# VectorE's norm, residual and router steps in smaller parts, and their places in the order of a fused two-layer kernel

## What is computed

```
x = x + tanh(g_xattn[0]) * L0_xattn(layernorm(x), ctx, mask)   # 16 heads, softmax, out projection,
                                                               # scaled, layernorm, gamma and beta
x = x + tanh(g_ffn[0])   * L0_ffn(layernorm(x))                # shared expert + 7 routed, top 3
x = x + tanh(g_xattn[1]) * L1_xattn(layernorm(x), ctx, ctx)    # gated recurrent cell as a masked product
x = x + tanh(g_ffn[1])   * L1_ffn(layernorm(x))                # block-quantised gate, up, down

# L0_xattn, per head:  p = clip(exp(q k / 4)) by key mask; o = (p v) / sum(p)
# L0_ffn:  gate_probas = softmax(x @ gate_w + gate_b)
#          top 3 of gate_probas + biases, weights normalised to sum 1
#          out = expert_shared(x) + sum_e w_e * (silu(x @ W1[e]) * (x @ Wg[e])) @ W2[e]
```

## Time and profile before

| | us |
|---|---|
| median of 3 runs (lowest, highest) | 495.32 (494.81, 496.61) |
| profiled execution, its own time | 496.37 |
| span of that execution | 494.6 |
| TensorE busy (share) | 381.1 (77%) |
| VectorE busy | 349.6 (71%) |
| ScalarE busy | 189.1 (38%) |
| GpSimd busy | 152.8 (31%) |
| chain that ended last: TensorE, VectorE, issue | 49%, 24%, 12% |
| mean granted clock of TensorE | 0.87 |

### The profile page before, as it was taken

One profiled execution on the slowest core, in us unless ns is written; L12 is line 12 of the kernel. 1 busy time (PEld: TensorE's weight loads), 2 busy tenths in 40 slices (PEclk: granted clock), 3 DMA queues, 4 the chain that ended last, 5 costly groups with the idle time before them and its releaser, 6 DMA issues.

```text
span 494.6 us, 6936 instructions
## 1 busy us (share of the span) xinstructions
PE 381.1 (77%) x2330; PEld 258.7 (52%) x2330; DVE 349.6 (71%) x857; ACT 189.1 (38%) x331; POOL 152.8 (31%) x147
## 2 busy tenths in 40 slices
PE   7899787799997697959767887979577478660745
PEld 3566454545556585848545555657353156440323
DVE  4586259257633989887976657577995976789895
ACT  4456424323313122603343545444004577640331
POOL 4029300028425445546325223233212020030240
PEclk9999997579998989979995999999697759966695
DMA  8900000003402203302986930907000670000001
GB/s 280 254 12 0 9 1 1 1 1 107 129 0 65 85 12 122 104 20 88 201 187 89 164 104 0 141 31 107 2 0 0 106 129 1 2 0 1 23 20 45
DMA packets 33714, 32.69 MB, mean 66 GB/s; under 512 B 3876, under 2 KB 32784, under 8 KB 33680
## 3 DMA queue, kind: packets, MB, share of 16 engines
q1 hardware_dynamic: 31088, 28.99, 26.4%
q0 software_dynamic: 992, 1.68, 1.2%
q10 hardware_dynamic: 1600, 1.57, 1.0%
HBM read 28.04 MB, written 4.19 MB: 65 GB/s over the span
## 4 chain that ended last, share of the span: by engine, by line
PE 49%; DVE 24%; issue 12%; ACT 6%; POOL 3%; DMA 3%; SPq 1%; DVEq 0%; ACTq 0%; POOLq 0%
PE bank L869 14%; PE bank L895 6%; PE bank L781 5%; PE bank L797 3%; PE bank L754 3%; PE bank L1005 2%; PE bank L969 2%; DVE mxraw L1610 2%; DVE mam L1452 2%; DVE tok L1262 2%; PE bank L765 1%; PE bank L917 1%; PE bank L954 1%; DVE probs L1537 1%; DMA qrep<-part_dram 1%
## 5 line engine op out<-in xcount | busy, mean ns | idle before, releaser
L895 PE MATMUL bank<-wexp,wT 128*128 128x256 f32 x192 | 53.9, 406 | 7.7 <-DVE x L1444 7.6
L869 PE MATMUL bank<-tok_r,probs_r 128*128 128x512 f32 x104 | 48.0, 462 | 11.6 <-DVE wT L1433 7.0
L1322 DVE TENSOR_SCALAR probs<-probs,hi 128x512 f32<-128x512 f32 x64 | 34.6, 592 | 28.8 <-ACT probs L1077 28.7
L663 POOL TENSOR_TENSOR wexp_r<-wexp,probs_r 128x1024 fp32r<-128x1024 f32 x13 | 31.2, 2403 | 60.3 <-ACT probs_r L1088 60.3
L1127 ACT ACTIVATE silu_sb<-bank 128x512 f32<-128x512 f32 x32 | 19.1, 597 | 77.1 <-PE bank L869 77.1
L1077 ACT ACTIVATE probs<-bank 128x1024 f32<-128x1024 f32 x32 | 32.2, 1025 | 41.1 <-PE bank L781 41.1
L591 POOL TENSOR_TENSOR mx_grid<-parts,bl 128x1024 bf16<-128x1024 fp8e4 x9 | 17.2, 1910 | 96.0 <-DVE parts L1613 96.0
L895 PEld LDWEIGHTS bank<-wexp,wT 128*128 128x128 f32 x192 | 37.1, 203 | 15.3 <-issue 10.5
L1537 DVE SCALAR_TENSOR_TENSOR probs<-bank,dexp 128x384 f32<-128x384 f32 x48 | 26.4, 554 | 24.0 <-PE bank L955 17.7
L869 PE MATMUL bank<-tok_r,wexp_r 128*128 128x512 f32 x104 | 42.7, 411 | 0.0
L781 PE MATMUL bank<-qrep,krep 32*128 32x256 f32 x256 | 35.8, 410 | 1.8 <-issue 1.0
(11 more groups left out here) (261 smaller groups left out, 895.9 us busy)
## 6 DMA issues: line engine op xcount, KB each, us to landing
wexp<-in_L_ffn_W SPq DMA_DIRECT2D x28, 256.0 KB, 4.1
krep<-part_dram SPq DMA_DIRECT2D x32, 128.0 KB, 6.6
qrep<-part_dram SPq DMA_DIRECT2D x32, 128.0 KB, 4.6
wexp<-in_L_ffn_Wg SPq DMA_DIRECT2D x14, 256.0 KB, 4.6
part_dram<-parts POOLq DMA_DIRECT2D x4, 384.0 KB, 3.0
part_dram<-parts SPq DMA_DIRECT2D x4, 384.0 KB, 3.3
x<-in_x ACTq DMA_DIRECT2D x2, 512.0 KB, 7.2
ctx<-in_ctx SPq DMA_DIRECT2D x2, 512.0 KB, 7.0
```

Of the source, the lines that this page charges most:

```text
L663: gp.tensor_tensor(low, raw, w_high[k % 2].bitcast(F32), ALU.subtract).then_inc(s["w_low_ready"], 1)
L869: mm = pe.matmul(bank[:, bk, :], lhs, rhs, start=(kk == 0 and q == 0), stop=(kk == KC - 1 and q == len(terms) - 1))
L895: mm = pe.matmul(bank[:, 2 + pair, D * t:D * t + D], hid[k % 2][m][:, col:col + P], wexp[:, k % WR, 2, m, :], start=(m == 0), stop=(m == 1))
L1322: ins = v.tensor_scalar(w, w, hi[:, 2 * b + kc:2 * b + kc + 1], EM50, ALU.min, ALU.max)
```

## The change

No instruction's work is changed. VectorE's steps are cut up: ln_in keeps the statistics and ln_root gets the inverse root; delta_in gives its root to delta_root; delta_out gives its first pass to delta_mid; route keeps its first three instructions, route_rank has the softmax and the comparisons, route_weigh the rest; VectorE's part of score becomes a step clamp of its own, directly behind score everywhere but in groups 4 and 5. There all eight score steps come ahead of the clamps, with delta_mid, delta_out, ln_in 2, ln_root 2 and ln_out 2 between them; values 4 comes behind gate 0. x_split 0 moves ahead of the experts on ScalarE, and on GpSimd ahead of the copies of the gate weights and of the context. The woven chains have more and smaller side steps, so that delta_in 1, ln_in 3, ln_in 4, cell_in 0, cell_mid 0, cell_out 0 and ln_in 6 come up to one TensorE step earlier, and the roots, route_rank 1 and route_weigh 1 later. cell_in 0 thereby comes ahead of w_split 15, which has parts on ScalarE and GpSimd as well.

```
@@ -123,7 +123,7 @@
     st = lambda name, *ix: [(name, i) for i in (ix or (0,))]
-    plan = st("key_masks") + st("ln_in", 0) + st("turn", 0, 1, 2) + st("bias_turn") + st("project", 0) + st("turn", 3)
+    plan = st("key_masks") + st("ln_in", 0) + st("ln_root", 0) + st("turn", 0, 1, 2) + st("bias_turn") + st("project", 0) + st("turn", 3)
     plan += st("ln_out", 0) + st("project", 2) + st("turn", 4, 5) + st("mask_turn") + st("project", 1)
@@ -137,7 +137,7 @@
         if g - 1 >= first:
             late[1] = late[1] + st("values", g - 1)
             late[2] = st("values_copy", g - 1)
-        return [st("score", 4 * g + j) + late[j] for j in range(4)]
+        return [st("score", 4 * g + j) + st("clamp", 4 * g + j) + late[j] for j in range(4)]
     def attention_end(g):
         w = g // 2
@@ -146,15 +146,15 @@
                 st("turn2", g) + st("turn2_copy", g), st("wo", w)]
     first = attention(0)
-    plan += flat(first[:2]) + st("project", 3) + st("turn", 6, 7) + st("ln_in", 1) + flat(first[2:]) + st("v_project", 0)
+    plan += flat(first[:2]) + st("project", 3) + st("turn", 6, 7) + st("ln_in", 1) + st("ln_root", 1) + flat(first[2:]) + st("v_project", 0)
     plan += st("ln_out", 1) + flat(attention(1)) + st("v_project", 1) + st("tanh")
     plan += weave(attention(2), st("turn", 8, 9)) + weave(attention(3), st("turn", 10, 11))
     end = attention_end(3)
     plan += end[0] + end[1] + st("project", 4) + end[2] + st("project", 5) + end[3] + end[4] + st("project", 6) + end[5]
-    second = [st("project", 7) + st("v_project", 2, 3)] + attention(4, 4) + attention(5, 4) + attention(6, 4)
-    second = [second[q] + second[q + 1] for q in (0, 2, 4, 6)] + second[8:]
-    plan += st("delta_in", 0) + second[0] + st("delta_out", 0) + second[1] + second[2] + st("ln_in", 2) + second[3] + st("ln_out", 2)
-    plan += st("xt", 0) + second[4] + st("route", 0)
+    plan += st("delta_in", 0) + st("delta_root", 0) + st("project", 7) + st("v_project", 2, 3) + st("score", 16, 17)
+    plan += st("delta_mid", 0) + st("delta_out", 0) + st("score", 18, 19) + st("ln_in", 2) + st("score", 20, 21) + st("ln_root", 2)
+    plan += st("ln_out", 2) + st("score", 22, 23) + st("clamp", 16, 17, 18, 19) + st("xt", 0) + st("route", 0) + st("x_split", 0)
+    rest = [st("values", 4) + st("clamp", 20, 21) + st("values_copy", 4) + st("route_rank", 0), st("clamp", 22, 23) + st("route_weigh", 0)]
     def expert(k, mx=None):
@@ -176,11 +176,11 @@
         return now + (st("accumulate", 2 * k - 1) if k else [])
-    plan += weave(flat([expert(k) for k in range(3)]), second[5:] + attention(7, 4) + attention_end(7))
-    plan += st("w_split", 3) + st("x_split", 0)
-    chain = st("delta_in", 1) + st("delta_out", 1) + st("ln_in", 3) + st("ln_out", 3)
+    plan += weave(flat([expert(k) for k in range(3)]), rest + attention(6, 4) + attention(7, 4) + attention_end(7))
+    plan += st("w_split", 3)
+    chain = st("delta_in", 1) + st("delta_root", 1) + st("delta_mid", 1) + st("delta_out", 1) + st("ln_in", 3) + st("ln_root", 3) + st("ln_out", 3)
     plan += weave(expert(3, 0) + expert(4, 1) + expert(5, 2), chain)
-    plan += weave(expert(6, 3), st("xt", 1) + st("route", 1)) + st("x_split", 1) + expert(7, 4)
+    plan += weave(expert(6, 3), st("xt", 1) + st("route", 1)) + st("x_split", 1) + weave(expert(7, 4), st("route_rank", 1) + st("route_weigh", 1))
     def cells(g, first=0):
@@ -205,13 +205,13 @@
         return [st("cell_values", g) + st("cell_values_copy", g), st("turn3", g) + st("cell_normalise", g)]
     def prepare(n):
-        return st("ln_in", 4 + n) + st("ln_out", 4 + n) + st("xt", 2 + n) + st("q_high", 2 * n, 2 * n + 1) \
+        return st("ln_in", 4 + n) + st("ln_root", 4 + n) + st("ln_out", 4 + n) + st("xt", 2 + n) + st("q_high", 2 * n, 2 * n + 1) \
             + st("gate_rows", n) + st("q_split", 2 * n) + st("gate_math", n) + st("q_split", 2 * n + 1)
     def finish(n):
-        return st("cell_in", n) + st("cell_mid", n) + st("cell_out", n) + st("ln_in", 6 + n) + st("ln_out", 6 + n)
-
-    plan += expert(8, 5) + weave(expert(9, 6), prepare(0)[:2] + [[]] + prepare(0)[2:4]) + weave(expert(10, 7)[:6], prepare(0)[4:]) + expert(10, 7)[6:8] + st("turn_gates", 0)
+        return st("cell_in", n) + st("cell_mid", n) + st("cell_out", n) + st("ln_in", 6 + n) + st("ln_root", 6 + n) + st("ln_out", 6 + n)
+
+    plan += expert(8, 5) + weave(expert(9, 6), prepare(0)[:3] + [[]] + prepare(0)[3:5]) + weave(expert(10, 7)[:6], prepare(0)[5:]) + expert(10, 7)[6:8] + st("turn_gates", 0)
     plan += weave(expert(10, 7)[8:] + flat([expert(k, k - 3) for k in range(11, 14)]), flat([cells(g) for g in range(4)]) + cells_end(3))
     plan += weave(expert(14, 11) + expert(15, 12), finish(0))
     plan += st("out", 30, 31) + st("quantise", 0) + st("accumulate", 30, 31)
@@ -234,7 +234,7 @@
         return [now("last", 4, True) + early, part(0), part(1) + late, now("quantise", 0) + now("down", 3, True)]
     ready = prepare(1)
-    plan += st("q_turn", 0) + ready[:2] + flat(stage_d(0)[:3]) + ready[2:] + flat(stage_d(0)[3:]) + st("turn_gates", 1)
+    plan += st("q_turn", 0) + ready[:3] + flat(stage_d(0)[:3]) + ready[3:] + flat(stage_d(0)[3:]) + st("turn_gates", 1)
     plan += flat(stage_d(1) + stage_d(2)[:3])
     plan += weave(flat([cells(g, 4) for g in range(4, 8)]), [[]] + stage_d(2)[3:]) + flat(cells_end(7))
     plan += weave(finish(1), stage_d(3)[:3]) + flat(stage_d(3)[3:])
@@ GpSimd's queue @@
...
                 gp.dma_start(part_dram[1, u].rearrange("a p t -> p a t"), parts[:, u, :, :]).then_inc(s["ck_stored"], 16)
-            gp.wait_ge(s["gate_loaded"], 16 * 14)
...
-            gp.wait_ge(s["pv_done"], 8)
-            for i in range(NT):
-                gp.tensor_scalar(vaug[:, i, 0:H * VS]
...
-            def w_split(k):
...
             def x_split(n):
...
+            x_split(0)
+            gp.wait_ge(s["gate_loaded"], 16 * 14)
...
+            gp.wait_ge(s["pv_done"], 8)
...
+            def w_split(k):
...
@@ -691,7 +692,7 @@
             steps = dict(w_split=w_split, x_split=x_split, mx_quantise=mx_quantise, q_split=q_split, cell_in=cell_in, quantise=quantise)
             for name, i in plan:
-                if name in steps:
+                if name in steps and (name, i) != ("x_split", 0):
                     steps[name](i)
@@ -1250,6 +1251,8 @@
                     m = seq.add(v.bn_aggr(mv[:, i, :], st[:, i, :]))
                 seq.wait(m)
                 seq.add(v.tensor_scalar(ve[:, k, :], mv[:, i0:i0 + TH, 1], LN_EPS, None, ALU.add))
+
+            def ln_root(k):
                 inverse_root(ri[:, k, :], ve[:, k, :], ru[:, 0, :], ru[:, 1, :])
             def ln_out(k):
@@ -1313,7 +1316,7 @@
                 seq.add(v.tensor_tensor(rs2[:, 1:2], rs2[:, 0:1], rs2[:, 0:1], ALU.mult))
                 seq.wait()
-            def score(u):
+            def clamp(u):
                 g, jj = u // 4, u % 4
                 _, _, b, _ = group(g)
                 v.wait_ge(s["exp_done"], u + 1)
@@ -1355,17 +1358,22 @@
                     seq.add(v.bn_aggr(mv[:, i, :], st[:, i, :]))
                 seq.wait()
                 seq.add(v.tensor_scalar(dve_[:, n, :], mv[:, i0:i0 + TH, 1], rs2[:, 1:2], LN_EPS, ALU.mult, ALU.add))
+
+            def delta_root(n):
                 inverse_root(dri[:, n, :], dve_[:, n, :], ru[:, 0, :], ru[:, 1, :])
                 seq.wait()
                 seq.add(v.tensor_scalar(dri[:, n, :], dri[:, n, :], rs2[:, 0:1], None, ALU.mult))
+
+            def delta_mid(n):
+                i0 = TH * n
+                seq.wait()
+                v.wait_ge(s["gscaled"], 2)
+                for i in range(i0, i0 + TH):
+                    seq.add(v.scalar_tensor_tensor(tok[:, i, :], tok[:, i, :], mv[:, i, 0:1], lng[:, :], ALU.subtract, ALU.mult))
             def delta_out(n):
                 i0 = TH * n
-                seq.wait()
-                v.wait_ge(s["gscaled"], 2)
                 v.wait_ge(s["x_beta"], i0 + TH)
-                for i in range(i0, i0 + TH):
-                    seq.add(v.scalar_tensor_tensor(tok[:, i, :], tok[:, i, :], mv[:, i, 0:1], lng[:, :], ALU.subtract, ALU.mult))
                 seq.wait()
                 for i in range(i0, i0 + TH):
                     seq.add(v.scalar_tensor_tensor(x[:, i, :], tok[:, i, :], dri[:, n, i - i0:i - i0 + 1], x[:, i, :], ALU.mult, ALU.add))
@@ -1383,6 +1391,9 @@
                 seq.add(v.tensor_reduce(lgs[:, 0, :], lgt, AX.X, ALU.max))
                 seq.wait()
                 v.tensor_tensor(lg[:, 0, :, :], lgt, bc(lgs[:, 0, :]), ALU.subtract).then_inc(s["rexp_in"], 1)
+
+            def route_rank(n):
+                bc = lambda ap: ap.unsqueeze(2).broadcast_to([P, TH, NE])
                 v.wait_ge(s["rexp_out"], n + 1)
                 seq.add(v.tensor_reduce(lgs[:, 1, :], lg[:, 1, :, :], AX.X, ALU.add))
                 seq.wait()
@@ -1400,6 +1411,9 @@
```

(3 more changed lines are left out.)

61 lines of the change are left out of this document (35 added, 26 removed).

## The result

The changed kernel takes 482.64 us (median of four executions: 479.95, 480.16, 485.13, 485.56) beside 495.4 us before; the ratio is 0.974, with a 95% interval of 0.970 to 0.978. Its profiled execution took 480.16 us (span 478.3), against 496.37 before: 16.2 us less. The forecast was 480.8 for that execution and 479.7 for the median. The total is right; several of the parts are not, as the stretches show.

The account below looks back on a forecast made before the run. No engine bounds everywhere: TensorE from 104.5 to 152 us, VectorE in 159–197.3 and 339.1–365.4 us. Terms 6.4 - 0.5 + 4.0 + 1.5 + 5.4 + 1.4 - 2.6 = 15.6 us saved: 480.8 profiled, 479.7 median, range 471 to 487.

Parts of the forecast that it names:

- A and B: Attention's second end, 73 to 104.5 us: 6.4 us saved (4.4 to 13.5); then to 152 us: 0.5 us lost.
- C: Start of expert 3: x_low ready 2.3 us earlier, clock staying up; 4.0 us saved, 2.3 if the clock falls.
- D1: Experts 3 to 5, 159 to 197.3 us: half of VectorE's idleness goes, 1.5 us saved (4 lost to 5.5 saved).
- D2: Expert 6 and second routing, 197.3 to 216.1 us: TensorE's 5.28 us wait goes, 5.4 us saved (3.3 to 7.2).
- F: At ln_in 4: statistics go ahead of step 18's activation, ln_out 4 ends earlier; 1.4 us saved (0 to 1.7).
- E: cell_in 0 ahead of w_split 15: split queues later and mx_quantise 11 is locked once more; 2.6 us lost (0 to 5).
- The low clock case: Attention's end, main case: TensorE's clock is low, back at 96.0 us, and up ends at 98.1; 6.4 us saved.
- The rival's case: Attention's end: TensorE's clock stays up, 13.5 us saved instead of 6.4, giving 472.6 us; chance 0.18.
- B alone: From 104.5 to 152 us: x_split 0 on GpSimd can hold VectorE's clamps; 0.5 us lost (nothing to 1.2).
- The sign of the last line: Stated sign of being wrong: VectorE still full but its 4-element root operations at 1 to 2 us each, in numbers.
- the lock rival: 159 to 216.1 us: VectorE stands still through GpSimd's operations, 22 us added, 501.7 us at the most; main case keeps 0.51.
- expert gains vanish: VectorE's sum is the bound from 152 to 224 us; D1 and D2 give nothing, E 5: 489.0 us; chance 0.10.

Follow-up runs that it names:

- a_again: The changed kernel run again with nothing altered, for its spread: 486.03 us, ratio 0.982 to the kernel before.
- xsplit_only: The kernel before with x_split 0 alone moved, behind the first routing, on GpSimd ahead of the gate weights: 490.35 us, ratio 0.989.
- attn_only: The changed kernel's attention end and early x_split 0, with the expert chains placed as in the kernel before: 485.69 us, ratio 0.976.
- experts_only: The kernel before with only the changed kernel's new expert chains; old attention end and place of x_split 0: ratio 1.0007.
- combo: Changed kernel with pieces, ranking and weighing moved around GpSimd's runs, ln_in 4, cell_in 0, ln_in 6 in old places, spare TensorE matmuls: 475.28 us, ratio 0.960.
- dodge: The changed kernel with the seven pieces of the chain of experts 3 to 5 moved ahead of mx_grids: 484.82 us, ratio 0.978.
- before_again: The kernel before, unchanged, run once more with its profile: 497.1 us, one execution.
- nolock: The changed kernel without the first two of GpSimd's three operations of mx_quantise 0 to 2, result not right: 477.38 us, one execution.
- combo_nowarm: The same kernel as combo without the spare matmuls: 480.17 us, ratio 0.970.
- warm: The changed kernel with a spare matmul behind each of scores 16 to 23 and four ahead of the router's product: 482.29 us, ratio 0.974.

## Why the prediction was right, and where it was not

| term | forecast | measured, after (a_again) |
|---|---|---|
| A and B | 5.9 saved | 11.3 (6.4) saved |
| C | 4.0 saved | 4.0 (4.0) saved |
| D1 | 1.5 saved | 3.4 (3.4) lost |
| D2 | 5.4 saved | 0.9 (0.9) saved |
| F | 1.4 saved | 0.3 (0.3) lost |
| E | 2.6 lost | 0.6 (0.6) lost |
| in no term | 0 | 4.5 (4.4) saved |
| sum, by the stretches | 15.6 | 16.3 (11.4) saved |

**A and B** were right in mechanism: tok was ready at 81.70 (forecast 81.5), and the transposes waited for the scores alone. The low clock case was right in size: 6.4 in a_again (5.9 forecast). The rival's case was not met in full even by the lucky execution: 11.3 us of the 13.0 (13.5 less 0.5), with the clock still low for 3.4 us. (Halving the stated prices from 79.5 on gives an end at about 90.2, not 91.0, so that case was written 0.8 us too small as well.) What failed is that the clock was taken as one outcome with a chance; it differs from execution to execution. The forecast gave 0.67 to a low clock and 0.18 to a high one; two of ten executions were near 480. The profiled execution that gave 480.16 was of the rarer kind, and 4.5 us came where no term stood; these two together hid the failure of the expert terms. That the total of the profiled execution came out to 0.6 us is luck. The median of 482.64 and a_again's 486.03 are 2.9 and 6.3 us above the forecast. The early VectorE finish did not keep the clock up by itself: the fall at 77.3 us came inside the scores, without TensorE idle for longer than 0.46 us. The prediction tied the fall at 80.1 to TensorE's having stood idle from 79.5; a_again shows a fall without such idleness.

**B alone**: from the exponential of score 24 to step 5 it is 40.45 us against 42.18 before, and gate 1's four products (half of the 3.70 us at 91.32) moved out of it: 0.1 us lost instead of 0.5.

**C** was right to 0.1 us: TensorE's product at 140.59 starts 0.10 us behind the end of w_split 3 (138.14 + 2.35), GpSimd's only operation there. Timeline of TensorE in after:

```profile
140.59 0.47 PE L870 MATMUL bank<-tok_r,probs_r 128*128 128x512 f32 x1 [0.45 <-issue]
```

**D1** failed in one step: "splitting moves such instructions to other places, with the same odds". The idle rest did shrink by half as forecast (3.0 to 1.4 us). But VectorE's busy time grew by 4.9 us, and 4.9 less 1.6 is the 3.3 us lost. The odds were not the same, and could have been worked out from the list: each mx_grids starts GpSimd's run of three operations, and w_split follows it, some 6.2 us (149.78 to 155.91 in after) in which VectorE's operations on SBUF alone were held. The new weave put the root and delta_out behind mx_grids. (With the old order reached as early as in xsplit_only and attn_only, D1 was 39.8 and 40.2 us, so 0.8 to 1.2 us of the loss may belong to the arrival; experts_only has the 3.4 us without it.) The lower bound of the term (4 lost) held. The sign of the last line ("4-element root operations at 1 to 2 us each") is what came.

The Trainium skill, page "SBUF — State Buffer", section "Who interferes with whom", says that whoever comes first gets the shared ports for the whole instruction while the other is blocked entirely, and that the order of issue decides who is blocked, not the shape of the operation. The trace agrees: 128x4 operations took up to 2.24 us, until the GpSimd operation of 2.38 us ended. That rule, which the prediction left to the lock rival (chance 0.05) alone, carried the sign of D1.

**D2** was mis-sized. Timelines of VectorE and TensorE in after, where ranking and weighing went:

```profile
198.10 2.39 DVE L1402 TENSOR_TENSOR lg<-lg,lgs 128x28 f32<-128x28 f32 x1
...
209.46 2.33 DVE L1431 TENSOR_TENSOR cw<-lg,lgs 128x28 f32<-128x28 f32 x1
```
```profile
206.15 0.50 PE L870 MATMUL bank<-tok_r,probs_r 128*128 128x512 f32 x1 [2.50 <-DVE hid_x L1447]
...
213.48 0.50 PE L870 MATMUL bank<-tok_r,probs_r 128*128 128x512 f32 x1 [2.55 <-DVE wT L1447]
```

The wait of 5.28 us became two, of 2.50 and 2.55 us; VectorE's sum is 25.55 us in this stretch, 25.56 before. The estimate of 2 us coming back took the ranking alone and forgot the weighing and its lock. What remains is 0.9 us, with a granted clock of 1.00 instead of 0.89 in the window; the forecast had 2.0 us for the clock. (Its own terms, 7.3 less 2, give 5.3, not 5.4.) The "expert gains vanish" rival, given 0.10, describes the sizes of D1, D2 and F better than the main case did, but not its reason: VectorE's sum did not stay, it grew by the held time. combo put the ranking clear of GpSimd's run (0.19 us for the product of L1402 that took 2.39), and the stretch became no shorter (32.02 us). VectorE in combo:

```profile
180.40 2.31 DVE L1493 TENSOR_SCALAR mx_sc<-mx_top 128x16 f32<-128x16 f32 x1
193.38 2.09 DVE L1482 TENSOR_SCALAR mx_top<-mx_top 128x16 uint32<-128x16 uint32 x1
204.13 2.33 DVE L1436 TENSOR_TENSOR lg<-lg 128x28 f32<-128x28 f32 x1
```

Two operations of mx_quantise and one of the weighing were held instead. Taken together, D1 and D2 are 70.5 us before, 73.0 after, 68.2 in dodge and 67.3 in combo.

**F**: the transposes' wait fell from 1.70 to 0.54 us, as forecast. But the last statistics operation (L1253) was held 2.14 us, and step 18's first product waited:

```profile
220.81 2.14 DVE L1253 TENSOR_SCALAR ve<-mv 128x4 f32<-128x4 f32 x1
```
```profile
223.69 0.47 PE L870 MATMUL bank<-tok_r,probs_r 128*128 128x512 f32 x1 [2.02 <-DVE silu_sb L1441]
...
227.23 1.09 PE L843 MATMUL bank<-identf,tok 128*128 128x128 f32 x8 [0.54 <-DVE tok L1265]
```

**E** went as told: w_split 15 directly behind cell_in's product, and a second lock on mx_quantise 11 beside the one of the earlier trace rows. Timelines of GpSimd and VectorE in after:

```profile
327.68 2.39 POOL L690 TENSOR_TENSOR pvs<-tok,lsc 128x1024 f32<-128x1024 f32 x1 [9.44 <-DVE tok L1583]
330.02 2.35 POOL L673 TENSOR_TENSOR wexp_r<-wexp,probs_r 128x1024 fp32r<-128x1024 f32 x1
```
```profile
328.23 1.87 DVE L1468 TENSOR_SCALAR mx_top<-mx_top 128x16 uint32<-128x16 uint32 x1
330.13 2.27 DVE L1479 TENSOR_SCALAR mx_sc<-mx_top 128x16 f32<-128x16 f32 x1
```

It cost 0.6 us in the stretch, not 2.6. The granted clock was 0.94 there and 0.81 before, so part of the price is hidden under a better clock. The table separates the two: with 3.4 us of low clock in the stretch, the old place took 25.94 to 25.96 us (before_again, xsplit_only, attn_only) and the new one 26.88 to 26.90 (after, a_again, dodge, nolock). The new place thus costs 0.9 us.

**In no term**: from step 21 to 28 after gained 2.3 us with no change of order. The low clock there was 13.7 us long in both executions of before and 6.8 in after. xsplit_only, whose order there is that of before, has 6.8 us too and 72.95 us: so the new order isn't needed for it; that the earlier arrival is what did it was not tested. The other 2.1 us, behind quantise 0, stay open. The first execution of before had 10.2 us of low clock at 397.5 us where after had 3.4; but before_again had 3.4 there as well and still took 126.10 us, so the clock at that place seems to account for some 0.5 us only. Kernels with the new places of cell_in 0 and ln_in 6 take from 124.0 (nolock) to 127.3 us (experts_only) behind quantise 0, those with the old ones 126.1 to 126.8. Why the low stretches fall where they do stays open too.

## What to carry to other kernels

Before VectorE's small SBUF steps are moved, list GpSimd's unbroken runs of operations: of a step inside one, each instruction on SBUF alone can wait for a whole GpSimd operation (delta_out 6.25 us), while clear of the run it does not (1.67 us in dodge). With not an instruction changed this was worth 4.8 of 73.0 us in two stretches, of which 3.1 us were left at the end of the profile and none could be told in the median. Cut a step out of TensorE's wait only where VectorE has idle time behind it; where VectorE is full, one wait of 5.3 us comes back as two of 2.5. Read the granted clock of more than one execution before a gain or loss of 1% is put down to an order, and where a stretch that everybody waits for runs at a clock that wavers, try spare matmuls in TensorE's gaps: they gave 4.9 us between combo_nowarm and combo, though nothing clear between the changed kernel and warm.
